# VectorE's order inside one pipelined step: an output norm in two fused operations, and searches placed between dependent operations

## The reference, cut to what matters

```
# block 1: top-k cross attention, film, s4d convolution, feed-forward, norm
scores = einsum(x Wq, ctx Wk) / sqrt(32)             # 4 heads, 257 context rows
topv, topi = top_k(scores, 32); probs = softmax(topv) scattered back into a 257 row
c_t = mean_heads(probs) @ (ctx Wv)
xn  = layernorm(x) * (1 + g*scale_in) + g*shift_in   # scale, shift from c_t
y   = s4d(xn)  (a convolution over 32 tokens, here by a DFT), then film again
xt  = x + y;  xt = xt + gelu(layernorm(xt) W1) W2
x1  = layernorm(xt) * g_out + b_out                  # the output norm
# block 2: single head attention over 32 tokens;  x2 = x1 + attention(norm(x1))
# block 3: top-2 of 8 experts;                    out = x2 + sum_e gate_e * expert_e(norm(x2))
```

## Time and profile before

| what | value |
|---|---|
| median of 3 runs | 602.14 us (600.91 to 603.63) |
| the profiled execution | 601.02 us, of which the profile's span is 599.2 us |
| TensorE busy | 550.1 us, 92% of the span |
| VectorE busy | 497.5 us, 83% |
| ScalarE busy | 292.6 us, 49% |
| GpSimd busy | 282.3 us, 47% |
| DMA queue | 41.51 MB, 20.7% of 16 engines' time |
| mean granted TensorE clock | 0.972 |

### The profile page before, as it was taken

The page is one execution under the profiler, slowest core; times in us unless marked ns, Lnnn a source line. Parts: engine busy times, 40 slices in busy tenths (PEclk is TensorE's granted clock), DMA queues, the critical chain, the costliest instruction groups (busy, mean ns, idle before and its releaser), DMA issues.

```text
span 599.2 us, 13091 instructions
## 1 busy us (share of the span) xinstructions
PE 550.1 (92%) x4558; PEld 406.0 (68%) x4558; DVE 497.5 (83%) x1761; ACT 292.6 (49%) x768; POOL 282.3 (47%) x662
## 2 busy tenths in 40 slices
PE   2588487999999999999999999999999999989877
PEld 2344264868686877778786868686868687766755
DVE  7997877689898999989899999898999899966433
ACT  3132242364646565555546463646464656434522
POOL 7755147525445362626363636353544535251621
PEclk9998898899999999999999999999999999989988
DMA  8488203030403030301213030303030300000000
GB/s 269 76 311 340 79 1 122 2 113 2 131 2 131 1 128 4 100 33 59 73 25 108 19 113 20 112 19 114 2 131 2 131 1 10 2 10 2 9 1 18
DMA packets 17957, 42.33 MB, mean 71 GB/s; under 512 B 2770, under 2 KB 9570, under 8 KB 17380
## 3 DMA queue, kind: packets, MB, share of 16 engines
q1 hardware_dynamic: 17892, 41.51, 20.7%
HBM read 39.37 MB, written 2.13 MB: 69 GB/s over the span
## 4 chain that ended last, share of the span: by engine, by line
PE 77%; DVE 3%; issue 3%; POOL 3%; ACT 2%; POOLq 0%; DVEq 0%
PE D L1136 9%; PE BB L1136 9%; PE BB L1159 8%; PE D L1153 8%; PE SS L1116 4%; PE SS L1122 3%; PE PC L1277 3%; PE PC L1316 2%; PE PC L1279 2%; PE BB L1237 2%; PE BB L1238 2%; PE BB L1272 2%; PE BB L1271 2%; PE PC L1219 2%; PE BB L1254 2%
## 5 line engine op out<-in xcount | busy, mean ns | idle before, releaser
L553 POOL TENSOR_SCALAR var_in<-mv 128x1 f32<-128x1 f32 x64 | 14.0, 219 | 238.4 <-DVE mv L782 140.9
L817 DVE MATCH_REPLACE8 work<-top,work 128x257 f32<-128x257 f32 x192 | 77.5, 412 | 0.0
L1136 PE MATMUL D<-ang,e_w 128*128 128x128 f32 x512 | 73.6, 292 | 0.0
L1136 PEld LDWEIGHTS D<-ang,e_w 128*128 128x128 f32 x512 | 65.6, 202 | 10.1 <-issue 10.1
L811 DVE MAX8 top<-work 128x8 f32<-128x257 f32 x192 | 71.1, 412 | 0.0
L1153 PE MATMUL D<-expw,ang 128*128 128x256 f32 x256 | 66.0, 389 | 1.2 <-ACT ang L628 0.9
L1136 PE MATMUL BB<-ang,w 128*128 128x128 f32 x512 | 65.0, 282 | 0.9 <-ACT ang L709 0.9
L1136 PEld LDWEIGHTS BB<-ang,w 128*128 128x128 f32 x512 | 62.1, 196 | 3.1 <-ACT ang L709 1.3
L628 ACT ACTIVATE ang<-BB,cols 128x128 f32<-128x128 f32 x128 | 36.5, 367 | 50.9 <-PE BB L1136 50.9
L1159 PE MATMUL BB<-expw,ang 128*128 128x256 f32 x256 | 57.9, 379 | 0.0
L649 ACT ACTIVATE expo<-SS,nmax,srs 128x257 f32<-128x257 f32 x64 | 32.7, 562 | 51.5 <-DVE work L797 51.3
(11 more groups left out here) (262 smaller groups left out, 1238.5 us busy)
## 6 DMA issues: line engine op xcount, KB each, us to landing
ctx_n<-in_ctx_n SPq DMA_DIRECT2D x16, 768.0 KB, 4.3
ctx_t<-in_ctxT SPq DMA_DIRECT2D x16, 514.0 KB
ctx_t<-in_ctxT SPq DMA_DIRECT2D x16, 257.0 KB
xT<-in_xT SPq DMA_DIRECT2D x16, 128.0 KB, 2.5
x_all<-in_x SPq DMA_DIRECT2D x4, 512.0 KB, 9.2
out<-out_sb SPq DMA_DIRECT2D x16, 128.0 KB, 1.7
ctx_l<-in_ctx_l SPq DMA_DIRECT2D x16, 96.0 KB, 5.1
w<-in_W SPq DMA_DIRECT2D x1, 1024.0 KB
```

Of the source, the lines that this page charges most:

```text
L817: V.match_replace(work[:, 2 * q + k, :], top[:, 2 * q + k, 8 * r8:8 * r8 + 8], work[:, 2 * q + k, :], TAKEN).then_inc(chains["taken"], 1)
L1136: ins = MM(bank[:, 128 * m:128 * m + 128], w[:, k, at:at + 128], xs[:, 128 * k:128 * k + 128], start=k == 0, stop=k == 1)
```

## The change: what it does

The arithmetic of the output norm is regrouped: `(xt2 - mean) * gout` in one operation and `u * rstd + xb_c` in another, in place of three. The first is issued between `maxima(a, 0)` and `take(a, 0)`, the second after `z`. `find8` and `take8` get a choice of rows, and `probs` is split into `prob_of` and `sums`. Instructions of one chain are then separated by instructions of another. All other arithmetic is as before, and only VectorE's list changes.

```diff
                 if b:
                     top8(b, 1, 3)
-                    probs(b, 1)
+                    prob_of(b, 1, 0)
+                    prob_of(b, 1, 1)
                 if c:
                     V.tensor_tensor(xt2, xt_b, B1[:, 0:D], ALU.add)
+                if b:
+                    sums(b, 1)
+                if c:
                     bn_stats(bn[1]); bn_aggr(mv[1]) -> st1_v
                 if a:
                     maxima(a, 0)
+                if c:
+                    wait(dve, s["st1_v"], one(c))
+                    V.scalar_tensor_tensor(u_c, xt2, mv[1][:, 0:1], gout, ALU.subtract, ALU.mult)
+                if a:
                     take(a, 0)
                 if dd:
-                    link(logit)
+                    logit                     # dots_a, inorm_g
+                if a:
+                    find8(a, 0, 1)
+                if dd:
                     best
                 if a:
-                    top8(a, 0, 1)
+                    take8(a, 0, 1)
+                if dd:
+                    nbest
+                if a:
+                    find8(a, 0, 2)
                 if b:
                     z
                 if c:
                     wait(dve, s["rs1_g"], one(c))
-                    V.tensor_scalar(u_c, xt2, mv[1][:, 0:1], rstd[1][:, 0:1], ALU.subtract, ALU.mult)
-                if dd:
-                    nbest
-                if c:
-                    V.tensor_tensor(u_c, u_c, gout, ALU.mult)
-                    V.tensor_tensor(x1, u_c, xb_c, ALU.add)
-                    stats(2, x1, c, "st2_v")
+                    V.scalar_tensor_tensor(x1, u_c, rstd[1][:, 0:1], xb_c, ALU.mult, ALU.add)
                 if dd:
-                    link(pg); link(rsum_d); gate
-                if a:
-                    find8(a, 0, 2)
+                    pg
+                if c:
+                    bn_stats(bn[2], x1)
+                if dd:
+                    rsum_d
+                if c:
+                    bn_aggr(mv[2]) -> st2_v
+                if dd:
+                    gate
                 if b:
                     xf (2)
                 if c:
                     xl2
+                if a:
+                    take8(a, 0, 2, (0,))
                 if b:
                     had (2)
                 if a:
                     maxima(a, 1); take(a, 1)
                 if dd:
                     gated(range(0, 2))
-                if a:
-                    take8(a, 0, 2)
                 if b:
-                    link(yb *= B1[0:D]); link(yb += B1[D:2D]); xt; bn_stats; bn_aggr
-                if a:
-                    find8(a, 0, 3)
+                    yb *= B1[0:D];  take8(a, 0, 2, (1,));  yb += B1[D:2D]
+                    find8(a, 0, 3, (0,));  xt;  find8(a, 0, 3, (1,));  bn_stats;  bn_aggr
                 ...
                 if a:
                     take8(a, 0, 3)
+                    find8(a, 1, 1)
                 if c:
                     x2
-                    stats(3, x2, c, "st3_v")
-                if a:
-                    probs(a, 0)
-                    top8(a, 1, 1)
+                    prob_of(a, 0, 0);  bn_stats(bn[3]);  prob_of(a, 0, 1);  bn_aggr(mv[3]) -> st3_v
+                if a:
+                    sums(a, 0)
+                    take8(a, 1, 1)
```

More of the change, by code:

```diff
@@ L276, in build @@
         s = {n: sem(n) for n in names}
-        chains = {n: sem("self_" + n) for n in "tm g0 g1 g2 g3 len top taken u xhat best".split()}
+        chains = {n: sem("self_" + n) for n in "tm g0 g1 g2 g3 len top taken u xhat best y gate bn2 bn3".split()}
         ld_x = [sem(f"ld_x{k}") for k in range(4)]
@@ L802, in top8, with find8 @@
                 take8(a, q, r8)
-            def find8(a, q, r8):
-                for k in range(2):
+            def find8(a, q, r8, ks=(0, 1)):
+                for k in ks:
                     if r8 == 1:
@@ L829, in probs @@
                 V.reciprocal(rsum_row[:, 2 * q:2 * q + 2], psum_row[:, 2 * q:2 * q + 2]).then_inc(s["rsum_v"], 1)
+            def probs(a, q):
+                prob_of(a, q, 0)
+                prob_of(a, q, 1)
+                sums(a, q)
             def step(a, b, c, dd):
@@ L865, in step @@
                     V.tensor_tensor(xt2[:, :], xt_b[:, :], B1[:, 0:D], ALU.add).then_inc(s["xt2_v"], 1)
+                if b:
+                    sums(b, 1)
+                if c:
                     wait(dve, s["xt2_v"], one(c))
-                    stats(1, xt2[:, :], c, "st1_v")
+                    link(V.bn_stats(bn[1][:, :], xt2[:, :]))
+                    V.bn_aggr(mv[1][:, :], bn[1][:, :]).then_inc(s["st1_v"], 1)
                 if a and a.n == 3:
@@ L876, in step @@
                     wait(dve, s["inorm_g"], one(dd))
-                    link(V.scalar_tensor_tensor(logit[:, :], dots[:, NE:2 * NE], inorm[:, :], dots[:, 0:NE], ALU.mult, ALU.add))
+                    V.scalar_tensor_tensor(logit[:, :], dots[:, NE:2 * NE], inorm[:, :], dots[:, 0:NE], ALU.mult, ALU.add).then_inc(chains["best"], 1)
+                if a:
+                    find8(a, 0, 1)
+                if dd:
+                    wait(dve, chains["best"], dd.count(2, 1))
                     V.max(best[:, :], logit[:, :]).then_inc(chains["best"], 1)
                 if a:
-                    top8(a, 0, 1)
+                    take8(a, 0, 1)
+                if dd:
+                    wait(dve, chains["best"], dd.count(2, 2))
+                    V.tensor_scalar(nbest[:, :], best[:, 0:1], -1.0, None, ALU.mult).then_inc(s["nbest_v"], 1)
+                if a:
+                    find8(a, 0, 2)
                 if b:
@@ L970, in step @@
                     V.tensor_tensor(x2[c.p][:, :], x1[:, :], C0[:, 0:D], ALU.add).then_inc(s["x2_v"], 1)
+                if a:
+                    prob_of(a, 0, 0)
+                if c:
                     wait(dve, s["x2_v"], one(c))
-                    stats(3, x2[c.p][:, :], c, "st3_v")
+                    V.bn_stats(bn[3][:, :], x2[c.p][:, :]).then_inc(chains["bn3"], 1)
                 if a:
-                    probs(a, 0)
-                    top8(a, 1, 1)
+                    prob_of(a, 0, 1)
+                if c:
+                    wait(dve, chains["bn3"], one(c))
+                    V.bn_aggr(mv[3][:, :], bn[3][:, :]).then_inc(s["st3_v"], 1)
+                if a:
+                    sums(a, 0)
+                    take8(a, 1, 1)
                 if dd:
```

55 lines of the change are left out of this document (31 added, 24 removed).

## The result

| | before | after |
|---|---|---|
| median of 20 runs each, taken together | 602.94 us (600.82 to 605.85) | 607.61 us (605.25 to 612.24) |
| ratio, with its 95% interval | | 1.0082 [1.0063, 1.0101] |
| the profiled execution's span | 599.2 us | 606.5 us |
| TensorE busy | 550.1 us | 555.2 us |
| VectorE busy | 497.5 us | 476.8 us |

The change takes 20.7 us of work off VectorE and makes the kernel 0.8% slower. The forecast was +2.0 us, 604.1, with a range to 607.6. The sign was right; what came is +4.7 us (602.94 to 607.61), more than twice the forecast, and the median lies just past the end of the range.

What follows compares the result with a forecast made beforehand. TensorE, busy all of a full step, was taken as the bound. 0.69 + 1.01 + 1.3 - 0.2 - 0.79 = +2.0 gave 603.0 us profiled, 604.1 for the median; range 602.6 to 605.6, or 600.4 to 607.6 for 8 in 10.

Steps and rivals of the forecast that it cites:

- Its own sign of being wrong: A full step of 32 us or more, or no growth of step 1's wait for hn, would refute the prediction.
- Its sign of the collision: u at about 0.6 us beside GpSimd's L589 would show that they collide; 0.42 would refute it.
- Step 1: Pipeline fill: one take and two searches lengthen the chain to hn, +0.69 us, bounds 0.3 to 1.35.
- Step 2: Pipeline fill: two searches and the output norm's first half stand before z, +1.01 us, bounds 0.8 to 1.4.
- Step 17: Drain, last tile's output norm: fewer operations follow GpSimd's rstd, -0.79 us, bounds -0.6 and -0.9.
- Step 16: Drain, TensorE's 2.0 us wait for wsel: VectorE's earlier arrival gives back 0.2 us, bounds -0.55 and +0.1.
- steps 3 to 15: The 13 full steps: three terms giving 0.10 us per step, +1.3 us together, bounds -0.9 and +5.2.
- z, +0.14: Full steps: u, delayed 0.2 to 0.3 us by L589, makes z late, so TensorE waits 0.14 us at L1226.
- wsel at L1201, -0.07: Full steps: TensorE's hidden 0.07 us wait for GpSimd's wsel at L1201 goes away.
- L1151, +0.03: Full steps: the chain to hn, +0.69 us, makes TensorE's L1151 0.03 us later, bounds 0 and 0.1.
- The first rival: u and L589 collide in full in every step: +4.6 us, 606.7 us, slower; chance 0.25.
- The clock: The granted clock falls after some long TensorE waits; a changed wait can bring or spare a spell, 1.7 us.

Runs made afterwards that it cites:

- e6: The changed kernel with only the take put back ahead of the chain to hn, the two searches staying in it; 605.00 us, ratio 1.0044.
- e4: The changed kernel with GpSimd's x plus bias (L589) moved behind its norm 1; 608.96 us, ratio 1.0089.
- e2: The changed kernel with the take and two searches taken out of the chain to hn and put back where they stood; 604.18 us, ratio 1.0039.
- e5: The changed kernel with the edits of e2 and e3 together; 600.15 us, ratio 0.9966.
- e8: The kernel of e5 with u, the first half of the norm, issued right after z; 600.84 us, ratio 0.9972.
- e9: The changed kernel with GpSimd's x plus bias replaced by a fill, and a longer fill in front of it; 606.8 us, one run.
- e10: The changed kernel with u alone issued right after z, the searches staying in front of z; 603.85 us, ratio 1.004.
- e3: The changed kernel with the pair of searches find8(a, 0, 2) put back behind the gate, after z; 602.37 us, ratio 1.0018.
- e1: The kernel before with the fused output norm alone, both operations behind z; 599.41 us, ratio 0.9951.
- e12: The kernel of e1 once more, on another set of runs; 602.22 us, ratio 0.9989.
- e11: The kernel of e4 once more; 608.91 us, one run.

## Why the prediction missed

Its own sign of being wrong came: a full step of 32.03 us, with 32 as the bound. Its sign of the collision couldn't tell anything: u takes 0.47 us beside L589 and 0.48 in step 2, away from it, where 0.6 and 0.42 were put.

**The prices held.** Step 1: `hn` +0.69 foretold, wait 7.3 foretold, 0.68 and 7.28 measured. Step 2: z +1.01 foretold, +1.05 measured (1.80 less 0.75). Its u took a slot of 0.39 instead of 0.35 (88.65 to 89.04). Step 17: -0.79 foretold, -0.70 measured (its 0.35 + 0.2 + 0.47 add up to 1.02 and not 1.04; 1.01 came). Step 16 gave nothing back (1.94 against 1.96), where -0.2 was taken. A take costs its 0.27 in the chain and two searches 0.42 (e6: 7.0; all three: 7.3). The strict reading of the Trainium skill's page "VectorE: DVE Perf Modes", section "The DRAIN you can't avoid", by which each insertion costs 0.45, doesn't hold here: from L951 to L956 are 0.74 us with a take between them, not 0.90.

**The part that failed is steps 3 to 15, in all three of its terms.** It summed 0.14 - 0.07 + 0.03 = 0.10 per step and 1.3 in all. Measured are 0.23 + 0 + 0.20 = 0.43 in a usual step and 5.54 in all (step 3 only 0.19, the step at 212 us 0.84).

- *z, +0.14.* Timing and mechanism were right: without a collision L785 to z was put at 3.12 + 1.01 + 0.3 = 4.43 and took 4.45 (e4), with 0.13 us to spare as foretold. The collision was put on the wrong operation. The one that meets L589 is not u but `nmax`, one place ahead. It was overlooked because it is 0.16 us long, and in the kernel before it was 0.16 beside L589 too; but it comes 0.34 us earlier there now, and a held operation waits for the other's end whatever its own length, so it lost 0.32, more than the 0.2 to 0.3 taken for u. 0.32 less the 0.13 to spare is 0.19: the 0.18 at L1254. With the 0.05 at L1255 the step feels 0.23 (e2: 31.83).
- *wsel at L1201, -0.07.* I read this wait in step 9, and step 9 was not a usual step: it is 31.65 us long (303.08 to 334.73), and the usual one of 31.60 has 0.57 us from L1194 to L1201. So it is in the kernel before in the step that begins at 208.28:

```profile
213.66 0.62 PE L1194 MATMUL D<-route,ang 128*128 128x16 f32 x4
214.23 0.64 PE L1201 MATMUL PC<-prob,wsel 128*32 128x257 f32 x8
```

  There was nothing to win (0.9 us of the sum), and e5 and e8 come out at 31.59, not at the 31.55 that I expected of them.
- *L1151, +0.03.* The lengthened chain was compared with the spare time correctly (0.69 against 0.64, L963 at 327.58 behind 326.94 in the earlier trace rows). Missed was that a chain that has moved runs beside other instructions: L408 meets `pT_blk` and takes 0.12 more. e6, with the chain 0.27 shorter, is clear of both. Together 0.68 + 0.12 - 0.64 = 0.16; TensorE felt 0.20 (0.19 in the shorter steps of e9 and e10), and 0.26 in those steps of e3, e4, e9 and e10 where L407 takes 0.39 to 0.40 us and not 0.34. That is the difference between their steps of 31.85 and 31.79. Beside L407 runs VectorE's `pn_c` (L977), at 0.24 us where L407 is long and 0.26 where it isn't.
- *One step, +0.35, not foretold.* In the step at 212 us TensorE waits for wsel, because the reciprocal stands behind xt2, which waits for GpSimd's xt_b. I had named that order and given it no price. No run changes that order alone:

```profile
216.91 0.42 DVE L866 TENSOR_TENSOR ang<-ang,BB 128x256 f32<-128x256 f32 x1 [1.64 <-POOL ang L607]
...
218.43 0.64 PE L1229 MATMUL PC<-prob,wsel 128*32 128x257 f32 x8 [0.29 <-POOL wsel L580]
```

Every kernel that keeps this order has that step (e5: 31.94 against 31.59; after: 32.44 against 32.03), e1 and e12 don't.

**The first rival was the nearest**, 606.7 us: a collision held to L589's end in every step, which decides once a step's wait passes 0.2. I gave it 0.25, because I took the two lists of instructions to meet "within 0.3 us" and let half of that count as a miss. Its +4.6 against the measured +4.7 is luck in part: it has 0.28 a step where 0.43 came, and the spans of the two profiles differ by 7.3 us. The bound of +5.2 for the thirteen steps was too low as well (5.54), and the range's top of 607.6 leaves no room even for it: 603.0 + 1.1 + 5.2 - 1.3 = 608.0.

**The clock** was named as what can move the total either way, by 1.7 us a spell. For single executions the traces bear that out (3.2 us between e11 and e4). It isn't shown to be what keeps e1 and e12 apart: at the same mean granted clock, 0.977, executions of e1 took 598.2 to 598.9 us and those of e12 601.7 to 602.8 (on another chip, where the kernel before was 0.7 us longer).

## What to carry to other kernels

When one engine is busy all the time, an order of another engine is read by its edges: for each result the bound engine takes, how early it is, and how much later the edit makes it. Filler of 0.33 us behind an operation that costs 0.45 when dependent saves 0.12 and moves that chain by 0.21. No filler is shown to have paid here: e5, which keeps those of x2, the gate and xt2, has the full step of the kernel before, and in step 17 the way from the rstd to the second statistic is 0.98 us without filler (e1) and 1.01 with it (after). The gain there is the fused norm's. Before an instruction is moved by some tenths of a microsecond, look at everything in the neighbourhood with two inputs in SBUF, the tiny ones first, and at what the other engine reads at that moment.

## What the runs showed of the hardware that I had not expected

- An operation of VectorE on 128x2 elements with two SBUF inputs, 0.16 us alone, is held to the end of a GpSimd instruction that reads two SBUF tensors: 0.48 us, ending within 0.02 us of it (after, e3, e5, e10). Where it starts 0.20 us behind that instruction and not 0.27, it takes 0.55: it pays what is left of the other. It works the other way too, on an instruction of one element per partition: L408 0.38 instead of 0.26 beside `pT_blk`. A fill by GpSimd doesn't hold it (e9).
- VectorE's 20.7 us less of busy time bought nothing: TensorE is busy for 31.98 of a full step's 32.03 us, and VectorE's longest idle stretches in the changed kernel end with TensorE (31.0 us in total before L926) or GpSimd (19.2 before L866).
- The same kernel can have two spells of low clock more near the end in one execution than in another (e11 and e4, which ran on two chips); that is 3.2 us of some 605, as much as most edits here were worth. On one chip, too, e4's kernel took 603.6 to 604.5 us four times and 608.5 to 610.7 eight times.
